# Splitting expert weights half a tile earlier, one shared split for the late tiles, and a final gather in four buffers

## The reference, cut to what matters

```
x = x + cross_attention(layernorm(x), ctx)
n = layernorm(x)
shared = gelu(n @ shared_up) @ shared_down              # one shared expert, 256 -> 1024 -> 256
probs  = softmax(n @ router_w)                          # 8 routed experts, 2 for each row
routed = sum over the 2 best e of  probs[e] * gelu(n @ routed_up[e]) @ routed_down[e]
out    = shared + routed + x
```

## Time and profile before

| what | us |
|---|---|
| median of three runs | 2426.49 (2423.14 to 2427.13) |
| the profiled execution, whole | 2424.05 |
| its span in the profile | 2421.9 |
| TensorE busy | 2283.5 (94%) |
| VectorE busy | 1819.4 (75%) |
| ScalarE busy | 1400.9 (58%) |
| GpSimd busy | 313.5 (13%) |

### The profile page before, as it was taken

How to read it: one execution, slowest core, us unless ns; L and a number is a source line. 1 busy time by engine, 2 the same in 40 slices (tenths; PEclk the granted TensorE clock), 3 DMA queues, 4 the chain that set the end, 5 groups by cost and what they waited for, 6 DMA issues and landing times. The chain is left out here.

```text
span 2421.9 us, 41489 instructions
## 1 busy us (share of the span) xinstructions
PE 2283.5 (94%) x13892; PEld 1583.9 (65%) x13892; DVE 1819.4 (75%) x2487; ACT 1400.9 (58%) x2088; POOL 313.5 (13%) x305
## 2 busy tenths in 40 slices
PE   3999999999999999999999999996899999988885
PEld 3565655555655655565555566564788898988884
DVE  4898889889789889888978978984435555566656
ACT  4676566567557557657656756753335555555552
POOL 2010000010001001000001000101750212111110
PEclk7999999999999999999999999997999999999997
DMA  6235235334424433523533442443653434355545
GB/s 238 75 103 175 73 97 168 97 89 143 123 72 125 144 93 100 178 70 98 169 95 89 143 123 73 126 142 130 245 184 106 140 128 139 114 179 173 173 178 174
DMA packets 150761, 319.84 MB, mean 132 GB/s; under 512 B 35168, under 2 KB 67552, under 8 KB 147360
## 3 DMA queue, kind: packets, MB, share of 16 engines
q1 hardware_dynamic: 139520, 283.74, 37.1%
q0 software_dynamic: 11040, 33.60, 3.7%
HBM read 199.27 MB, written 82.35 MB: 116 GB/s over the span
## 5 line engine op out<-in xcount | busy, mean ns | idle before, releaser
L739 ACT ACTIVATE probs<-scores 128x1024 f32<-128x1024 f32 x514 | 499.2, 1024 | 460.4 <-PE scores L584 415.8
L687 PE MATMUL pv_ps<-probs,v_nat 128*64 128x512 f32 x2048 | 495.9, 605 | 0.2 <-DVE probs L872 0.2
L976 DVE TENSOR_TENSOR p_sum<-p_sum,probs 128x1024 f32<-128x1024 f32 x384 | 469.4, 1222 | 6.7
L872 DVE TENSOR_SCALAR probs<-probs 128x2048 f32<-128x2048 f32 x257 | 317.6, 1236 | 169.2 <-ACT probs L739 168.9
L584 PE MATMUL scores<-q_split,k_split 64*128 64x512 f32 x3084 | 425.4, 407 | 1.3 <-issue 0.7
L584 PEld LDWEIGHTS scores<-q_split,k_split 64*128 64x128 f32 x3084 | 269.6, 184 | 228.9 <-issue 182.5
L1409 PE MATMUL hp<-xT,up 128*128 128x512 f32 (+1 forms) x1680 | 353.3, 353 | 40.6 <-DVE up L1540 38.5
L1429 PE MATMUL yp<-down,hid_split 128*128 128x256 f32 x2640 | 364.2, 289 | 22.7 <-DVE acc L1725 17.1
L1429 PEld LDWEIGHTS yp<-down,hid_split 128*128 128x128 f32 x2640 | 349.8, 194 | 44.9 <-issue 24.9
L1545 DVE TENSOR_TENSOR hid_split<-hid,hid_split 128x512 fp32r<-128x512 f32 x210 | 145.4, 692 | 299.8 <-ACT hid_split L1489 298.7
L1488 ACT ACTIVATE hid<-hp 128x512 f32<-128x512 f32 x220 | 131.5, 598 | 345.0 <-PE hp L1409 345.0
(11 more groups left out here) (198 smaller groups left out, 2259.8 us busy)
## 6 DMA issues: line engine op xcount, KB each, us to landing
kT_swap<-kT SPq DMA_DIRECT2D x264, 128.0 KB, 2.3
w<-wpack SPq DMA_DIRECT2D x66, 512.0 KB, 4.0
raw<-L_ffn_routed_up SPq DMA_DIRECT2D x27, 1024.0 KB, 4.7
raw<-L_ffn_routed_down SPq DMA_DIRECT2D x27, 1024.0 KB, 5.8
rden<-rden_rows SPq DMA_DIRECT2D x128, 128.0 KB, 2.9
ctx_parts<-stage SPq DMA_DIRECT2D x32, 512.0 KB, 3.2
ctxs<-ctx_parts SPq DMA_DIRECT2D x16, 1024.0 KB, 6.9
sorted_rows<-zero POOLq DMA_DIRECT2D x64, 162.5 KB, 2.7
```

Of the source, the lines that this page charges most:

```text
L687: last = pe.matmul(pv_ps[64 * head:64 * head + 64], v_nat[p // 2 % 2][:, j, cols:cols + 64], probs[:, j % PROBS, head], start=j == 0, stop ...
L739: act.activation(probs[:, j % PROBS], scores[j % 2][:], ACT.Exp, scale=float(HD) ** -0.5).then_inc(s_exp, 1)
L872: v.tensor_scalar(pr, pr, EXP_LO, EXP_HI, ALU.max, ALU.min).then_inc(s_clip, 2)
L976: v.tensor_tensor(to, to, probs[:, j % PROBS], ALU.add).then_inc(s_add, 1)
```

## The change

What it does, in four parts:

1. **Order of the weight split.** Each engine's body now gets tile t, the next n and the one after, m. At the chunks c = 0 to 3 of tile t the `down` weights of n are split, at c = 4 to 7 the `up` weights of m. The sequence of splits is the same, half a tile earlier. Since `up` of m goes to the buffer that t itself reads, ScalarE waits ahead of the first of them until all up products of t are done (`s_up` at `t.c0 + t.steps`).
2. **Late tiles.** Both late tiles read the same `up` and `down` buffers; the shared weights are loaded and split once for them, not twice.
3. **Gather.** Four buffers: the two old ones and the raw weight buffer that is free by then. The gather of batch b waits for batch b-4.
4. **Combine.** In halves of four instructions, one half in each of the steps f = 6 to 9 of the first late tile and f = 2 to 7 of the second (ten halves, batches 0 to 4); six halves follow behind the last tile.

The loops over the tiles are unrolled by one more pair at their ends. The diff, cut to its core:

```diff
-        gat = [t[:, 0:2 * QT * D].rearrange("p (t n d) -> p t n d", n=2, d=D) for t in pair]
+        gat = [t[:, 0:2 * QT * D].rearrange("p (t n d) -> p t n d", n=2, d=D) for t in pair + raw[1 - ROUTED % 2]]
+        GATS = len(gat)
...
         def late(n):
-            u = (ROUTED + n) % 2
-            return Tile(T=HEAD + ROUTED + n, c0=FT * (HEAD + BIG + n) + 4 * SMALL, u=u, wu=1 - u, r=ROUTED + n, k=(ROUTED + n) // 2,
+            return Tile(T=HEAD + ROUTED + n, c0=FT * (HEAD + BIG + n) + 4 * SMALL, u=(ROUTED + n) % 2, wu=1 - ROUTED % 2,
+                        r=ROUTED + n, k=(ROUTED + n) // 2,
                         batch=HEAD + n, parts=HEAD // 2)
...
+            first = [shared(b) for b in range(HEAD)] + [big(0, 0), big(0, 1)]
+            for b in range(HEAD):
+                body(*first[b:b + 3])
             with eng.Fori(0, BIG // 2 - 1) as k:
-                body(big(k, 0), big(k, 1))
-                body(big(k, 1), big(k + 1, 0))
+                body(big(k, 0), big(k, 1), big(k + 1, 0))
+                body(big(k, 1), big(k + 1, 0), big(k + 1, 1))
...
+        def own_weights(t):
+            return t is not None and t.r is not None and t.batch != HEAD + 1
...
+            sp.wait_ge(s_wlo, FT * ROUTED - FT // 2)
+            load_up(ROUTED % 2, shared_up[0])
+            sp.wait_ge(s_wlo, FT * ROUTED)
+            load_down(ROUTED % 2, shared_down[0])
             for n in range(LATE):
-                r = ROUTED - 2 + n
-                sp.wait_ge(s_wlo, FT * r + FT + FT // 2)
-                load_up(r % 2, shared_up[0])
-                sp.wait_ge(s_wlo, FT * r + 2 * FT)
-                load_down(r % 2, shared_down[0])
...
             for b in range(B):
-                if b >= 2:
-                    sp.wait_ge(s_comb, b - 1)
+                if b >= GATS:
+                    sp.wait_ge(s_half, 2 * (b - GATS + 1))
...
+                if b >= GATS:
+                    store(b - GATS)
...
@@ ScalarE
-                    if n is not None and n.r is not None:
-                        c = (f - 2) * wide
-                        loads = weights_of(n)
+                    c = (f - 2) * wide
+                    if c < FT // 2 and own_weights(n):
                         if c == 0:
                             act.wait_ge(s_dn, t.c0)
-                            act.wait_ge(s_rawup[n.u], loads * 16 + 16)
+                            act.wait_ge(s_rawdown[n.u], weights_of(n) * 16 + 16)
+                        high_weights(n.u, n.wu, c + FT // 2, wide)
+                    if c >= FT // 2 and own_weights(m):
                         if c == FT // 2:
-                            act.wait_ge(s_rawdown[n.u], loads * 16 + 16)
-                        high_weights(n.u, n.wu, c, wide)
+                            act.wait_ge(s_up, t.c0 + t.steps)
+                            act.wait_ge(s_rawup[m.u], weights_of(m) * 16 + 16)
+                        high_weights(m.u, m.wu, c - FT // 2, wide)
...
@@ VectorE
-            COMBINE = ((0, 7), (0, 9), (1, 3), (1, 5), (1, 7))
+            COMBINE = [(0, f) for f in range(6, FT + 2)] + [(1, f) for f in range(2, FT)]
...
-                    if n is not None and n.r is not None:
-                        low_weights(n.u, n.wu, (f - 2) * wide, wide, n.r * FT + FT)
+                    c = (f - 2) * wide
+                    if c < FT // 2 and own_weights(n):
+                        low_weights(n.u, n.wu, c + FT // 2, wide, n.r * FT + FT)
+                    if c >= FT // 2 and own_weights(m):
+                        low_weights(m.u, m.wu, c - FT // 2, wide, m.r * FT + FT)
                     if rows_next and not n.half and f in (5, 6):
                         low_rows(n, t, f - 5)
```

More of the change, by code:

```diff
@@ L1189, in experts @@
         s_back, s_free = sem("f_back"), sem("f_free")
-        s_gat = [sem(f"f_gat{i}") for i in range(2)]
+        s_gat = [sem(f"f_gat{i}") for i in range(GATS)]
         s_half = sem("f_half")
@@ L1219, in tiles @@
         def tiles(eng, body):
-            for b in range(HEAD - 1):
-                body(shared(b), shared(b + 1))
-            body(shared(HEAD - 1), big(0, 0))
+            first = [shared(b) for b in range(HEAD)] + [big(0, 0), big(0, 1)]
+            for b in range(HEAD):
+                body(*first[b:b + 3])
             with eng.Fori(0, BIG // 2 - 1) as k:
-                body(big(k, 0), big(k, 1))
-                body(big(k, 1), big(k + 1, 0))
[L1226 to L1233, removed]
+                body(big(k, 0), big(k, 1), big(k + 1, 0))
+                body(big(k, 1), big(k + 1, 0), big(k + 1, 1))
+            body(big(BIG // 2 - 1, 0), big(BIG // 2 - 1, 1), small(0, 0))
+            body(big(BIG // 2 - 1, 1), small(0, 0), small(0, 1))
+            with eng.Fori(0, SMALL // 2 - 1) as k:
+                body(small(k, 0), small(k, 1), small(k + 1, 0))
+                body(small(k, 1), small(k + 1, 0), small(k + 1, 1))
+            last = [small(SMALL // 2 - 1, 0), small(SMALL // 2 - 1, 1), small(SMALL // 2, 0), late(0), late(1), None, None]
+            for n in range(5):
+                body(*last[n:n + 3])
+        def own_weights(t):
+            return t is not None and t.r is not None and t.batch != HEAD + 1
         assert BIG % 2 == 0 and SMALL % 2 == 1 and LATE == 2 and HEAD % 2 == 0
@@ L1418, in down_product @@
                         pe.wait_ge(s_y, t.T)
-                    if t.r is not None:
+                    if own_weights(t):
                         pe.wait_ge(s_wlo, t.r * FT + 2 * FT)
@@ L1449, in _, with body @@
                 up_product(shared(0), f)
-            def body(t, n):
+            def body(t, n, m):
                 rows_next = n is not None and n.parts is None
@@ L1465, in body @@
                     pe.wait_ge(s_part[n.u], 16 * n.parts + 16)
-                if n is not None and n.r is not None:
+                if own_weights(n):
                     pe.wait_ge(s_wlo, n.r * FT + (FT + FT // 2))
@@ L1677, in address, with combine, body @@
                 v.tensor_tensor(dest[n.u][:, 0:q], whither[:, 0:q], aside[:, 0:q], ALU.add).then_inc(s_dest, 1)
[L1679 to L1690, removed]
-            COMBINE = ((0, 7), (0, 9), (1, 3), (1, 5), (1, 7))
-            def body(t, n):
+            def combine(b, n):
+                if n == 0:
+                    if b >= HEAD:
+                        v.wait_ge(s_y, late(1).T)
+                    v.wait_ge(s_gat[b % GATS], 16 * (b // GATS + 1))
+                else:
+                    v.wait_ge(s_half, 2 * b + 1)
+                for t in range(QT):
+                    q = b * QT + t
+                    last = v.scalar_tensor_tensor(acc[:, q], gat[b % GATS][:, t, n], gate[n][:, q:q + 1], acc[:, q], ALU.mult, ALU.add)
+                last.then_inc(s_half, 1)
+            COMBINE = [(0, f) for f in range(6, FT + 2)] + [(1, f) for f in range(2, FT)]
+            def body(t, n, m):
                 wide = 2 if t.half else 1
@@ L1713, in body @@
                     if is_late(t) and (t.batch - HEAD, f) in COMBINE:
-                        b = COMBINE.index((t.batch - HEAD, f))
-                        combine(b).then_inc(s_comb, 1)
+                        half = COMBINE.index((t.batch - HEAD, f))
+                        combine(half // 2, half % 2)
                 if t.batch is not None:
                     if n is None:
[L1718 to L1721, removed]
+                        for half in range(len(COMBINE), 2 * B):
+                            combine(half // 2, half % 2)
+                        v.wait_ge(s_half, 2 * B)
                     v.wait_ge(s_dn, t.c0 + t.steps)
```

17 lines of the change are left out of this document (10 added, 7 removed).

## The result

The changed kernel takes 2369.91 us (median; 2369.02 to 2371.03) against 2425.05 for the kernel before beside it: a ratio of 0.9773, with a 95% interval of 0.9756 to 0.9790. The prediction was 2371, from a sum of 2369.6 for the profiled execution; that execution took 2369.83, its span is 2367.7.

A forecast was written before the change was run, and what follows sets the result against it. TensorE is busy 94% of the span, so only its gaps and the end can be won. 2424.05 - 50.4 + 12 + 0.9 - 4.8 - 2.3 - 9.8 = 2369.6; predicted median 2371, range 2364 to 2377 (0.66).

The forecast's parts named there:

- Small tiles: Fifteen small tiles bounded by TensorE alone take 177.6 us against 228.06: 50.4 gained, if nothing else comes late.
- the rows: In small tiles VectorE's low rows are done at 3.3 us, TensorE asks at 4.3: one us is left.
- A: Small tiles find a new bound (VectorE's rows, an address wait, a late load), each us costing 14: 2385; chance 0.16.
- D: Split not earlier in effect, small tiles keep their 2.1 us waits, only the end gains: 2420; chance 0.03.
- Big tiles: New TensorE wait for low rows, 0.9 us late, 1.0 for each of twelve tiles: 12 lost.
- the cost of restarting behind the wait: In big tiles, a product behind a wait takes 0.1 us more, 1.70 against 1.59.
- rival B: The wait in the big tiles is hidden or smaller: 2359; chance 0.05.
- Rival E: Slower: the new gap in each big tile makes the granted clock fall there, 2435 at 0.81; chance 0.02.
- The fifth shared tile: First up chunks come ahead of the addition into acc: one chunk, 0.6, and some clock, at most 0.9 us lost.
- The end: From the first late product on, parts 2 to 4 gain 4.8, 2.3 (if the clock stays up) and 9.8 us.
- Gathers: First four, issued together, land in issue order; the first comes 2 to 4 us before its half combine; no tail waits.
- Rival C: Gathers land together and the tail's waits stay in part: 5 to 10 us more, 2378; chance 0.08.

The follow-up runs named there:

- e4: Changed kernel, but in small tiles VectorE does the rows behind the low_weights of f = 2: 2448.41 us against 2489.25 for the kernel before.
- e3: Changed kernel, but in big tiles VectorE does the low rows ahead of that step's low_weights: 2422.97 us against 2489.25 for the kernel before.
- e5: Changed kernel with big tiles' low rows ahead of low_weights and the acc addition directly behind hidden: 2353.57 us against 2424.96 for the kernel before.
- e3b: e3 a second time, on another chip: 2423.62 us, 65.6 less than the kernel before beside it, ratio 0.9755.
- e2: Parts 2 to 4 alone, weight split in the old order: 2476.47 us, 12.8 less than the kernel before, ratio 0.9952.
- e2b: e2 a second time, on another chip: 2475.98 us against 2489.23 for the kernel before, ratio 0.9954.
- e1: Kernel before with part 1 alone, the earlier weight split: 2447.07 us, 42.2 less than the kernel before, ratio 0.9836.
- e1b: e1 a second time, on another chip: 2447.61 us, 41.6 less than the kernel before beside it, ratio 0.9840.
- e8: Kernel before with part 2 alone, late tiles sharing one split: 2486.97 us against 2489.23 for the kernel before, ratio 0.9997.
- e6: Changed kernel with two gather buffers in place of four: 2377.91 us against 2424.96 for the kernel before, 8.0 more than the changed kernel.
- second set: The runs e1b, e2b, e3b and e8, on chips where the kernel before takes 2489.23 us.
- e7: Changed kernel with whole combines in place of halves: 2375.76 us against 2424.96 for the kernel before, 5.9 more than the changed kernel.

## Why the prediction was right, point by point

**Small tiles.** Worked out 177.6, measured 177.48. The step that carried it was to count the stage as products alone and then to look for what is late next; the closest was the rows, with 1.0 us. e4 bears that room out: its low rows start 2.88 us behind the start of that step's `hidden` and not 1.32, and TensorE waits 0.69 us, so the room was 0.9. Rivals A and D are out: the changed kernel has no wait of any name in this stage. One reading was incomplete: TensorE's waits in the small tiles before were not one line. Beside the 29.0 us for `up` stand 2.8 for `down`, fourteen times, and 2.2 ahead of the late tiles, which make up the 34.0 us idle. The sum was not hurt, since the 50.4 was worked out from the length of the stage and not from its waits; the order takes these waits away as well.

**Big tiles.** The wait was forecast at 0.9 us, twelve times, and is 0.87 to 0.91 ten times and about 0.6 twice. The cost was set at 12; from the first down product of the sixth shared tile to the first small tile it took 13.0 more (2126.29 - 1812.18 against 2112.77 - 1811.65). What was too small is the cost of restarting behind the wait: put at 0.1, in fact about 0.25, since the eleven big-tile periods between 1838.19 and 2126.29 took 12.1 us more than before (288.10 against 276.02), and their waits make only 9.4 of it. The rows show what was left out. Without a wait the next product starts before the one ahead of it has ended: the down product at 1851.84 lasts 1.61, and the up product follows 1.44 behind it. Behind a wait this overlap of 0.17 is lost too, beside the 0.1 by which the product is longer. e4's fourteen waits cost the same on top: 12.9 us for 9.4 idle. e3 shows the cause, rival B is out. Rival E is out as well: twelve waits of 0.9 us left the granted clock at 1.00.

**The fifth shared tile.** At most 0.9 was forecast; TensorE's wait there went from 0.38 to 0.98, and e5 takes it back to 0.38.

**The end.** 16.9 forecast, 17.1 measured (81.07 against 63.93), and piece by piece: 4.9 up to the second late tile's first down product, 31.8 us behind the first late product (4.8 and 31.9 forecast); 2.2 from there to the point where the last `hidden` is done, 16.2 us (2.3 and 16.1 forecast); and 10.0 behind it (9.8 forecast). The 2.3 stood under the condition that the clock stays up, and this was luck in part: behind the same wait of 2.0 us it stayed up in this trace and in e3's, and fell in those of e3b and e4, for 1.5 us.

The prediction also put all of the end down to parts 2 to 4, and the runs do not. e2 and e2b give these parts 14; e1 and e1b give the order 3.1 us of the end in both, and up to 2 more in one. The step that misplaced it is the one that starts the count at the first late product. The slow stretch that opens the late tiles and their wait for `down` (0.79 us; 0.83 in e2) are what the old order of the split leaves behind, so they belong to part 1. The total was right because both parts were there.

**Gathers.** Four were in flight together, and VectorE waited for none. They were issued at 2315.4, 2315.7, 2316.2 and 2316.7, two into `pair` and then two into `raw` (SyncE's rows in order of time; the length takes in the pause to the next):

```profile
2315.37 0.80 SPq L1330 DMA_DIRECT2D pair<-returned_rows  x2
2316.22 1.23 SPq L1330 DMA_DIRECT2D raw<-returned_rows  x2
```

Issue to landing, shortest, median and longest, of the four gathers into `pair`:

```profile
DMA to landing us min/median/max: 5.1/6.0/8.4
```

And of the four into `raw`:

```profile
DMA to landing us min/median/max: 5.8/8.8/12.4
```

The first four took 5.1, 8.4, 10.5 and 12.4 us in the order of their issue, so they landed one behind the other at about 2320.5, 2324.1, 2326.7 and 2329.1. The first, 5.1, is hardly more than the 4.9 of the earlier trace rows, and it was there 3.7 us before the first half combine at 2324.14 wanted it (2 to 4 forecast); the price of sharing fell on the later ones, which are wanted later. The last gather took 7.1 (7.3 forecast). Rival C is out. The Trainium skill (DMA: Bandwidth & Descriptors, Queues, rings and completion order) has each engine take the descriptors of a ring in their order; these landings agree with it.

**The sum.** Forecast 54.4 less, measured 54.2 less in the profiled executions. The terms that were off (1 too little lost in the big tiles, 0.3 too much in the fifth shared tile, 0.2 too little gained both in the small tiles and at the end) nearly cancel. The step from this sum to the median was not worked out: the prediction names 2.4 us between the profiled execution and the median and adds 1.4. The changed kernel's median lies 0.1 above its profiled execution, so 2371 came out 1.1 too high, and the sum 0.2 too low.

## What to carry to other kernels

A wait that is added to one engine is paid by what stands behind it in the queue of the next: list, for each new wait, the instructions queued behind it on the engine that it delays, and put those with the nearest reader first (e3: 12.9 us in its stage for exchanging two instructions; e5: 16.3 in all with a second exchange). Work that one step can hand to the half step before it takes a wait away without making anything faster, as long as the room of the next to be late is worked out as well. An edit can be worth next to nothing alone and still be needed: e8's gain can't be told from none, but four gather buffers in place of two are worth 8 (e6), and the raw buffer that it frees holds two of them. Before a difference of 1 or 2 us is credited to an edit, count the slow stretches in both traces.

## What the runs showed of the hardware that was not expected

On the chips of e1 to e4 and of the second set, every kernel lost about 64 us in the shared tiles, while GpSimd wrote the sorted rows. In e3's trace TensorE issues single products with gaps that no engine ended, and then waits 40.85 us; ScalarE and VectorE are idle too, and the profile names nothing on this core that ended their waits ("remote" or "issue"), while GpSimd goes on issuing its transfers:

```profile
1731.38 0.59 PE L1444 MATMUL yp<-down,hid_split 128*128 128x256 f32 x3 [1.15 <-issue]
...
1801.33 0.60 ACT L1503 ACTIVATE hid<-hp 128x512 f32<-128x512 f32 x1 [26.95 <-remote]
...
1801.87 2.90 PE L1444 MATMUL yp<-down,hid_split 128*128 128x256 f32 x12 [40.85 <-DVE acc L1745]
```

On the chips of the first comparison and of e5 to e7 none of this is seen with the same code. What holds the engines there stays open. It does not bear on the change: behind that stretch e3's waits are those of e5's trace but for the addition into `acc`.

The granted clock did not follow the gaps in a simple way either. Waits of 2.0 to 2.1 us in every small tile left it at 0.96, with a slow stretch behind about every second one (six of fourteen in the kernel before, eight in e8). Waits of 0.69 us in each (e4) were followed by no slow product among the small tiles. The same wait of 2.0 us at the second late tile was followed by one in e3b and e4 and by none in e2, e2b, e3, e6 and the changed kernel, and the waits of 3.67 (e8) and 4.27 (before) by products of 2.90. What decides between the two stays open; by these rows, and as an estimate, a time worked out from waits alone is good to about 1.5 us for each wait of 2 us.
